# One projection for keys and values, and eight filter iterations spread over five steps, in a fused image and text kernel

## The reference, cut to what matters

```python
# filter, 10 times
q = max(q - 0.5 * (du_rows * vf1 + du_cols * vf0), 0)
Tq = div(vf1 * q, vf0 * q)
u = sigmoid((o - Tq) / 0.5)
# fusion, for each sample of 384 rows
xn = layernorm(x)
q = xn @ Wq.T + bq           # 8 heads of 32
k = xn @ Wk.T + bk           # 2 groups of 32
v = xn @ Wv.T + bv           # 2 groups of 32
p = softmax(q k^T / sqrt(32) inside the window, with the sink)
y = x + (p v) @ Wo.T + bo
h = relu(layernorm(y) @ W_fc.T) ** 2
out = y + spikes(h @ W_proj.T) / 5
```

## Time and profile before

| | |
|---|---|
| median of three runs | 1094.4 us (1092.45 to 1096.61) |
| the profiled execution | 1095.0 us, of which 1093.0 are the profile's span |
| PE busy | 983.3 us, 90% |
| DVE busy | 903.6 us, 83% |
| ACT busy | 633.3 us, 58% |
| POOL busy | 98.2 us, 9% |
| chain that ended last | PE 53%, DVE 34%, ACT 6%, issue 4% |

### The profile page before, as it was taken

How to read it: one execution, slowest core, us unless ns; L and a number is a source line. 1 busy time by engine, 2 the same in 40 slices (tenths; PEclk the granted TensorE clock), 3 DMA queues, 4 the chain that set the end, 5 groups by cost and what they waited for, 6 DMA issues and landing times.

```text
span 1093.0 us, 18757 instructions
## 1 busy us (share of the span) xinstructions
PE 983.3 (90%) x7168; PEld 748.8 (69%) x7168; DVE 903.6 (83%) x1318; ACT 633.3 (58%) x2097; POOL 98.2 (9%) x149
## 2 busy tenths in 40 slices
PE   3689989989999988988998897879999999999997
PEld 2467777767777776776776775656666767777765
DVE  4999999999999999999999998659999963543442
ACT  2666766766766666676676664426454454735533
POOL 6100000000000000001000011010000010000000
PEclk9699999999999999999999999979999999999999
DMA  7500000200000200000200000000000010000000
GB/s 172 228 1 2 1 30 11 85 13 1 2 30 10 79 1 20 1 30 10 98 1 1 20 1 1 1 10 1 25 1 25 4 41 11 16 25 2 15 1 29
DMA packets 13690, 28.89 MB, mean 26 GB/s; under 512 B 2721, under 2 KB 9249, under 8 KB 12321
## 3 DMA queue, kind: packets, MB, share of 16 engines
q1 hardware_dynamic: 13216, 26.64, 7.2%
q0 software_dynamic: 384, 1.05, 0.5%
HBM read 22.44 MB, written 5.24 MB: 25 GB/s over the span
## 4 chain that ended last, share of the span: by engine, by line
PE 53%; DVE 34%; ACT 6%; issue 4%; POOL 1%; DMA 1%; SPq 0%; POOLq 0%; ACTq 0%; DVEq 0%
PE ps_t L587 10%; PE ps_t L596 8%; PE ps_t L792 5%; PE ps_s L485 4%; DVE neg_max L1446 3%; PE ps_m L803 3%; PE ps_s L536 2%; DVE f L1418 2%; PE ps_t L546 2%; PE ps_t L492 2%; DVE f L1440 2%; ACT hidT L1026 2%; DVE f L1422 2%; DVE f L1421 2%; DVE f L1410 2%
## 5 line engine op out<-in xcount | busy, mean ns | idle before, releaser
L960 ACT ACTIVATE prob<-ps_s,neg_max 128x128 f32<-128x128 f32 x512 | 180.6, 380 | 52.2 <-DVE neg_max L1446 52.2
L587 PE MATMUL ps_t<-hT_f,w 128*128 128x256 f32 x512 | 141.2, 423 | 34.4 <-ACT hT_f L972 17.8
L587 PEld LDWEIGHTS ps_t<-hT_f,w 128*128 128x128 f32 x512 | 100.3, 206 | 62.5 <-ACT hidT L1026 24.7
L596 PE MATMUL ps_t<-w,hidT 128*128 128x256 f32 x512 | 125.7, 383 | 0.0
L968 ACT ACTIVATE probT<-ps_t 128x512 f32<-128x512 f32 x128 | 77.3, 604 | 82.3 <-PE ps_t L546 51.0
L960 ACT ACTIVATION_READ_ACCUMULATOR prob<-ps_s,neg_max 128x1 f32 x512 | 112.9, 220 | 0.0
L596 PEld LDWEIGHTS ps_t<-w,hidT 128*128 128x128 f32 x512 | 90.9, 190 | 12.0 <-issue 3.0
L792 PE MATMUL ps_t<-km,w_fc 128*128 128x384 f32 x256 | 93.0, 499 | 1.0 <-ACT km L1134 1.0
L1026 ACT ACTIVATE hidT<-ps_t,b 128x256 f32<-128x256 f32 x128 | 55.0, 492 | 59.5 <-PE ps_t L587 59.5
L546 PE MATMUL ps_t<-ident,prob 128*128 128x128 f32 x512 | 81.9, 284 | 5.5 <-ACT prob L960 3.2
L546 PEld LDWEIGHTS ps_t<-ident,prob 128*128 128x128 f32 x512 | 64.0, 147 | 28.9 <-issue 12.4
(11 more groups left out here) (171 smaller groups left out, 1968.0 us busy)
## 6 DMA issues: line engine op xcount, KB each, us to landing
w<-in_w SPq DMA_DIRECT2D x8, 1024.0 KB, 4.9
w_attn<-in_w_attn SPq DMA_DIRECT2D x4, 768.0 KB, 4.5
out<-w SPq DMA_DIRECT2D x7, 384.0 KB, 2.4
o_all<-in_o SPq DMA_DIRECT2D x4, 512.0 KB, 10.1
filtered<-f_out SPq DMA_DIRECT2D x4, 512.0 KB, 2.6
x<-filtered SPq DMA_DIRECT2D x8, 256.0 KB, 2.7
vf<-in_vf SPq DMA_DIRECT2D x4, 256.0 KB
w_attn<-in_w_attn SPq DMA_DIRECT2D x4, 256.0 KB, 3.0
```

The source lines that it names most:

```text
L587: last = mm(ps_t[:, 0, D * (m % 2):D * (m % 2) + D], w1[:, c, P * m:P * m + P], hT_f[:, c], start=(c == 0), stop=(c == KC - 1))
L596: last = mm(ps_t[:, 0, D * t:D * t + D], hidT[:, m, P * t:P * t + P], w2[:, m], start=False, stop=(m == MC - 1), skip_group_check=True)
L960: last = A(prob[:, n % 2, hh], ps_s[n % 2][:, hh], ACT.Exp, scale=-1.0, bias=neg_max[:, n % 2, hh:hh + 1], accum_out=den)
```

## The change

Three things are changed, all in the fusion. First, `fuse_keys` now makes keys and values of both groups in one product of 128 rows (two halves of the depth, so 2 products of 384 columns instead of 4): rows 0 to 63 are keys, rows 64 to 127 values. `keys_biased` writes the 64 key rows twice, into both halves of `kT_f`; a new `values_in` on ACT copies the value rows out to `vT_f`, and `fuse_values` turns them back by six transposes instead of 12 products. The heads' order in the query weights is changed so that the scores read the two halves. The zeroed border of 64 columns moves from `xnT` to `vT_f`. One transfer fewer loads the weights. Second, the eight filter iterations lie 2, 1, 2, 1, 2 in steps 0 to 4. Third, the order of the calls is written anew in all steps, with its own order `fuse_late` for steps 5 to 7.

```diff
+FUSE_ITERS = [2, 1, 2, 1, 2, 0, 0, 0]
+FUSE_MID = 4
...
             def fuse_keys(n):
                 pe_.wait_ge(s["f_xnT"], n + 1)
-                for m in range(FKV):
-                    for c in range(KC):
-                        last = mm(quad[2 + m][:, 0:TOK], wk_f[:, c, m], xnT[:, c, WIN:], start=(c == 0), stop=(c == KC - 1))
+                for c in range(KC):
+                    last = mm(quad[2][:, 0:TOK], wkv_f[:, c], xnT[:, c], start=(c == 0), stop=(c == KC - 1))
                 last.then_inc(s["f_k_ps"], 1)
 
             def fuse_values(n):
-                pe_.wait_ge(s["f_k"], n + 1)
+                pe_.wait_ge(s["f_vT"], n + 1)
                 for w in range(2 * TT):
-                    for c in range(KC):
-                        last = mm(quad[3][:, 64 * w:64 * w + 64], xnT[:, c, WIN * w:WIN * w + P], wv_f[:, c], start=(c == 0), stop=(c == KC - 1))
+                    last = tr(quad[3][:, 64 * w:64 * w + 64], vT_f[64:, WIN * w:WIN * w + P], ident[64:, 64:])
                 last.then_inc(s["f_v_ps"], 1)
...
             def keys_biased(n):
                 act.wait_ge(s["f_k_ps"], n + 1)
-                for m in range(FKV):
-                    last = A(kT_f[:, m, WIN:], quad[2 + m][:, 0:TOK], ACT.Identity, bias=bk_f[:, m:m + 1])
+                for hb in range(2):
+                    last = A(kT_f[64 * hb:64 * hb + 64, WIN:], quad[2][0:64, 0:TOK], ACT.Identity, bias=bk_f[0:64])
                 last.then_inc(s["f_k"], 1)
+
+            def values_in(n):
+                act.wait_ge(s["f_k_ps"], n + 1)
+                A(vT_f[64:, WIN:], quad[2][64:, 0:TOK], ACT.Copy).then_inc(s["f_vT"], 1)
...
-            for n in range(1, B):
-                fuse_step(n, TEXT_ITERS + ITERS_IN_BLOCK * n)
+            for n in range(1, FUSE_MID + 1):
+                fuse_step(n, TEXT_ITERS + sum(FUSE_ITERS[:n]), FUSE_ITERS[n])
+            for n in range(FUSE_MID + 1, B):
+                fuse_late(n)
```

More of the change, by code:

```diff
@@ L167, in build @@
         bq_f = sb("bq_f", [P, KC])
[L168 removed]
+        bk_f = sb("bk_f", [P, 1])
         bv_f = sb("bv_f", [P, FKV * HD])
@@ L445, in fuse_step, with fuse_late @@
             def fuse_step(n):
+                scale_x(n + 1)
+                scale_y(n)
+            def fuse_late(n):
                 if n + 1 < B:
@@ L893, in fuse_step @@
                 fuse_out(n, 1)
+                ff_out(n - 1, 1, range(3, 4))
                 fuse_out(n, 2)
                 fuse_out(n, 0)
-                ff_out(n - 1, 1, range(3, 4))
-                if it < SLOTS * PAIRS // 2:
+                ff_out(n - 1, 2, range(0, 1))
+                turn_x(n + 1)
+                ff_out(n - 1, 2, range(1, 3))
+                if its > 1:
                     rows_above(it + 1)
-                ff_out(n - 1, 2, range(0, 1))
+                fuse_keys(n + 1)
@@ L1065, in block_step @@
                     keys_biased(0)
+                    values_in(0)
                 rden_out(a, 1)
@@ L1136, in x_out @@
             def x_out(n):
-                both([xnT[:, c, WIN:] for c in range(KC)], quad[2:4], s["f_xnT_ps"], n, s["f_xnT"])
+                both([xnT[:, c] for c in range(KC)], quad[2:4], s["f_xnT_ps"], n, s["f_xnT"])
             def o_out(n):
```

392 lines of the change are left out of this document (248 added, 144 removed).

## The result

The changed kernel takes 1062.7 us (median of 4 runs, 1059.5 to 1067.9) against 1093.4 us of the kernel before beside it: ratio 0.9722, 95% interval 0.9671 to 0.9772. Run once more beside the last experiments it took 1058.8 us, ratio 0.9714 (0.9663 to 0.9764). The forecast was 1064. The profiled execution took 1059.5 us, the shortest of its four; against the profiled 1095.0 of before that is -35.5, of which 2.35 lie ahead of the fusion, which starts at 661.61 instead of 663.96.

What follows compares the result with a forecast made beforehand. DVE bounds the two-iteration steps, PE those without iterations, neither step 0. Step 0 -14.7, steps 1 to 5 -11.6, step 6 -3.3, step 7 -1.7 make -31.3 from 1095.0: 1063.7, said as 1064, range 1051 to 1079.

Steps and rivals of the forecast that it cites:

- The signs: Wrong if steps 1, 3 exceed 47 us, DVE idles over 3 us in step 2 or 4, clock falls steps 2-7.
- Step 0: First fusion step, 67.8 us and bound by neither engine: 14.7 us less through waits, clock and PE work.
- named wait: At the end of step 0, the 4.65 us wait ahead of `turn_x2` goes.
- the keys' wait: At the end of step 0, the 1.14 us wait for the copied keys goes, now behind the queries.
- the half clock inside the step: In step 0's values and queries, the lower clock goes if PE's waits shrink: 3.5 us.
- the late wait: Rival: in step 0 `norm_y` comes late, so 4.65 and 3.5 us are not won: 1072 us; 3 in 100.
- Transposes: In each sample's projection, six replace 24 value products and take 0.66 us, so values save 1.97 us of PE.
- Steps 1 to 5: Steps 1 and 3 44.3 us each, 2 and 4 50.9 each, 5 43.6: together 234.0 against 245.6, -11.6.
- the first rival: More overlap: step 0 gains 16 us, two-iteration steps with empty DVE queue take about 48: 1055 us; 20 in 100.
- Step 6: Late fusion step without iterations, bound by PE: 3.3 us less.
- step 7: Last fusion step, projects nothing; `fuse_out` stands two parts of `ff_out` earlier: 1.7 us less.
- The lost clock: Rival: PE's clock falls at seven step borders, 5.4 us more each, 38 us in all: 1102 us; 5 in 100.

Runs made afterwards that it cites:

- a2: The full change with the filter iterations 2, 2, 2, 2 in steps 0 to 3 as before: 1065.1 us, ratio 0.9776.
- full change: The changed kernel with all three parts, against the kernel before: 1062.7 us, ratio 0.9722; beside the last experiments 1058.8 us, ratio 0.9714.
- p3: p2 plus the new order in step 0 and the tail, steps 1 to 7 in the old order: 1076.8 us, ratio 0.9869.
- p2: The kernel before with the 128-row projection and iterations 2, 1, 2, 1, 2, all queues in the old order: 1091.4 us, ratio 0.9986.
- d3: The full change with both the edits of d1 and d2: 1065.4 us, ratio 0.9761.
- q1: p3 with one swap on DVE, the second iteration's `divergence` ahead of `norm_y`: 1073.7 us, ratio 0.9831.
- b1: The full change with `divergence` put back behind `norm_y` on DVE in steps 2 and 4: 1068.6 us, ratio 0.9777.
- a3: The full change with steps 5 to 7 in the order of the earlier steps: 1068.0 us, ratio 0.9747.
- d1: The full change with ACT's second-iteration tanh behind the queries and PE's `rows_below` behind the first scores: 1063.5 us, ratio 0.9747.
- d2: The full change with the last two spike counts on DVE behind the next step's first maxima: 1065.6 us, ratio 0.9768.
- a1: The full change with the old separate products for keys and values: 1073.1 us, ratio 0.9811.
- p1: The kernel before with the 128-row projection alone, old queue orders and old iterations: 1091.6 us, ratio 0.9989.

## Why the prediction was right, and where it was not

**The bound.** Right for the kernel before: steps with two iterations DVE's, the others PE's. But "nothing PE saves shortens it" was too strong: 50.9 held 48.5 of DVE's work, 1.1 us of named waits and 1.2 of small gaps, and two iterations took 49.2 in a2 and 47.4 and 46.8 in the full change, part of their DVE work running on in the next step. After the change step 3 is no engine's: in its 47.20 us PE is idle for 3.5 and DVE for 10.9.

**The signs.** Of those that were to speak against the prediction one came: step 3 stayed at 47.20, above 47. Step 1 did not (44.75), DVE is idle for 1.5 us in steps 2 and 4, and the clock is 1.00 in steps 2 to 7. So the split of the time within steps 2 to 5 was wrong, and their sum came near (186.2 us, forecast 189.7).

**Step 0: -17.0, forecast -14.7.** The named wait, the keys' wait and the half clock inside the step went as written; the late wait (rival of 1072) did not come. p3 shows that it is this order: against p2 it takes 13.5 us off step 0, at a clock not wholly restored. What I gave to the clock, 3.5, is partly chance: in profiles with the same step 0 it lasts 50.8 at a clock of 1.00 (after twice, a2, d3) and 52.1 to 53.7 at 0.94 to 0.97 (p3, q1, b1, a3, d1, d2). In those the gain is 15.7 to 14.1, around the forecast, so the 2.3 us beyond it came with the better clock of the profiled execution. In a3 a low stretch begins behind a wait of 2.24 us for `qz`, and in the full change the same wait leaves the clock as it is. The full change, then a3:

```profile
664.45 0.38 PE L736 MATMUL ps_s<-mask,ident_h 128*128 128x512 bf16 x1 [2.24 <-ACT qz L1198]
664.76 1.10 PE L744 MATMUL ps_s<-kT_f,qz 64*64 64x128 f32 x32
```

```profile
667.90 0.55 PE L737 MATMUL ps_s<-mask,ident_h 128*128 128x512 bf16 x1 [2.24 <-ACT qz L1203]
668.38 1.99 PE L745 MATMUL ps_s<-kT_f,qz 64*64 64x128 f32 x32
```

The scores behind it take 1.0 us in the one and 1.9 in the other. The whole of it, 50.8 against 53.7, is up to 3 us of what a kernel's runs spread by.

**Transposes: 0.66 forecast.** Six take 0.52 (710.48 to 711.00) to 0.64 us (986.91 to 987.55), the value taken and not the issue gap's 0.17. The weight load's 107 ns of the Trainium skill ("TensorE: Matmul & The Clock Gate", section "LDWEIGHTS (loading the stationary operand)") is borne out at 0.64 (6 x 107 ns) and beaten at 0.52, 0.52 / 6 = 87 ns each.

**Steps 1 to 5: -14.7, forecast -11.6.** Step 1 44.75 (44.3), steps 2 and 3 94.6 (95.2), steps 4 and 5 91.6 (94.5). The pattern is that of the first rival, 47 for the full step and a longer one behind it. The waits for `qz` are 0.87 after step 1, 1.12 after step 2 and, ahead of step 5, 1.72 (forecast 0.65, 0.65, 1.2), ahead of steps 6 and 7 none as forecast. Right by parts that cancel.

**Step 6: -1.5, forecast -3.3; step 7: +0.5, forecast -1.7.** The two mis-sized terms of the fusion. PE's 3 us did go (a1), but in the forecast "every us of PE work taken out shortens it", and a1 to d3 show what stood close behind: the chain from the last `ff_out` over six spike counts to the first maximum, exponential and turn. It returns 1.0 to 1.2 us to each late step (a1 and d2 agree), at step 6 and 7 alike. Another 0.6 of step 6 shows only with the old products, a1's 46.24 against 45.68 before; with the short projection the new order costs nothing there (44.22 against 44.43 in p1 and 44.05 in a3), so the two terms of step 6 can't be told apart cleanly. Step 7's own term, `fuse_out` two parts earlier, forecast at 1.7, shows as 0.86: the wait ahead of `turn_x2` falls from 1.56 to 0.70, and the rest of that path is DVE's and POOL's.

```profile
1027.01 0.87 PE L694 MATMUL ps_t<-ident,xn 128*128 128x128 f32 x6 [0.70 <-DVE xn L1662]
```

**The sum.** By profiles -17.0 - 14.7 - 1.5 + 0.5 - 0.5 (tail) - 2.35 (ahead of the fusion) = -35.5. The last of these is -4.85 of chance, as far as the fourteen profiles tell, and +2.50 of the change, the projection of sample 0, for which the forecast had 0.4 less (counted with step 0): the third mis-sized term, since the wait that the long products covered there was not looked for. Without the chance the sum is -30.7 against -31.3, and the medians say -30.7 too. The misses have both signs, up to 3 us each, so that the total is nearer than its parts is luck.

**The rivals.** The lost clock was given 5 in 100 and did not come in the full change. Its mechanism is real: p1, p2, p3, b1 and q1 show it at the borders behind the full steps (0.93 to 0.97 in the step that follows), and the full change itself at the end of the text part. My argument against it, that old waits of 1.3 us left the clock alone, was about the size of the waits and said nothing about what the shorter products would make of them. In the full change each border has one wait of at most 1.7 us and at most 0.4 besides; q1, with 1.1 and 1.7 at one border, lost the clock. How near the full change is to that was not measured. Theory 1 of p1, made in the manner of this sum, said 8 to 12 us and the chip gave 1 to 3: for the projection alone the same reasoning was wrong.

## What to carry to other kernels

Work taken from the bounding engine is worth what stands behind the next waits: a long product at a border was also the cover for a chain on three other engines (divergence, tanh, queries; or counts, maximum, exponential), and without a new order of those queues some 26 us of saved PE work (3.2 a sample) gave at most 3 us. So walk each chain that ends in PE's next instruction with the saved time taken away, and look at in-order queues for what stands ahead of the one operation that PE needs. Do it at every place where the work was, the first sample too: there the shorter product made this kernel 1.4 to 2.5 us slower. Judge parts of a change together: here they gave 1 to 3 and 20 us alone and 31 together.

## What was not expected of the hardware

- The granted clock fell to 0.50 behind waits of PE of 4.9 us (p1, p2), of 2.78 us with 1.24 behind it (b1) and of 1.09 us with 1.72 behind it (q1), and stayed at 1.00 behind single ones of 0.7 to 1.7 us at the borders of the full change. Behind one of 2.24 us it fell in some executions of the same instructions and not in others. In the kernel before it fell at about 719.5 us in step 0, where the last wait was only 1.14 us. So the length of one wait does not decide it. A wait of PE costs its length and, at times, some us more: the scores and the `ff_in` products behind q1's second such border take 6.2 us (907.37 to 913.55), those of the full change 3.7 (759.13 to 762.85).
- Steps 1 to 7 of the full change repeat between its two profiles within 0.03 us each; nearly all the spread of its runs (1057.6 to 1067.9) would then lie in the text part, step 0 and the tail, whose lengths differ between profiles (tail 28.7 to 31.6 us at 0.88 to 0.99).
